# Own buffers for each pair's rows, norm and projections, and fewer VectorE steps for norm, rotary, softplus and factors, in a two-layer network of scan, experts and two attentions

## The chip, the cores and the metric

The kernel runs on one core of one Trainium2 chip. The time is the device time of one execution in microseconds (us), taken as the median of several runs. All arithmetic is float32, apart from a few masks and one-hot tables in bfloat16. The engines are named as in the profile: PE is TensorE (PEld its weight loads), DVE is VectorE, ACT is ScalarE, POOL is GpSimd, and SP is SyncE, which issues most DMAs.

## The reference

The input is 16 sequences of 256 rows with 128 features. Cut to what matters, this is computed:

```python
xn = layernorm(x)
x = x + mamba(xn) + experts(xn)          # block 0
xn = layernorm(x)
x = x + arccos_attention(xn) + window_layers(xn)   # block 1

mamba:   xt = silu(conv4(xn @ in_proj)); dt, B, C = split(xt @ x_proj)
         dt = softplus(dt @ dt_proj + dt_b)
         h[t] = exp(dt*A)*h[t-1] + dt*B*xt;  y = sum_n h*C + D*xt     # 256 channels x 16 states
         out = (y * silu(z)) @ out_proj
experts: top-1 of 8, relu(x @ w1 + b1) @ w2 + b2, times the gate's probability
arccos_attention, 16 heads of 8:  q, k = l2norm(q), l2norm(k)
         s = (1 + arccos(clip(q @ k.T))) ** -3.2;  n_r, n_c = row and column sums of s
         p = s / (n_r * n_c);  p = p / max(sum(p), 1e-12);  out = (p @ v) @ w_out
window_layers, 2 layers, 8 heads of 64:  h = shift(x)   # second 64 features one row later
         q, k, v = h @ wqkv;  q, k = rotary(l2norm(q)*qs), rotary(l2norm(k)*ks)
         x = x + softmax(window 64)(q, k) @ v @ wo
         h = layernorm(shift(x))*g + b;  a, g = h @ w1;  x = x + (a*gelu(g)) @ w2
```

## The kernel before

**Tiling.** The 16 sequences are taken as 8 pairs of 512 rows. A pair goes through block 0 (a scan over its 512 rows for 2 groups of 128 channels and 16 states, in 16 steps of 2 states each, and the experts, in 46 tiles of 128 routed rows of all pairs) and then through block 1: the arccos attention of the pair in 8 blocks of 4 heads, and two window layers for each of the two sequences, called b = 0 and b = 1.

**What sets the order.** The work is cut into units such as `("m_scan", pair, 0, step)` or `("ln", layer, b, 0)`. A unit is a chain of stages, each on one engine; `STAGES` gives the time that a planner assumes for each, `all_units` gives a wished time (`want`) and the units that must come first, and `schedule` plays all engines through once before the program is built: whenever an engine is free it takes the offered unit with the earliest wish. The result is one fixed order per engine, and a fixed PSUM bank per unit. On the chip each engine walks through its list in that order and waits at semaphores; nothing is reordered there. So the assumed times and the dependencies change the order, but a wait that comes late on the chip holds everything behind it on that engine.

**Streams.** Block 1 has three streams that run beside each other: the arccos attention (`g_...` units, ACT lines L1235 to L1255 for its logarithms, tangents and powers, POOL line L1721 for a subtraction of 2048 columns, called `g_sub`), and the window layers of b = 0 and of b = 1. Beside them runs the scan of a later pair (`m_...` units, DVE lines L1416, L1422, L1428). The experts (`e_...`) run in the first part only.

**Names on which the change acts.** For pair i:

- `f_yg` (POOL, L1717) gathers the expert rows into `yg`, which is the same memory as `sq`, the squares of the window layers' q and k. It therefore waits until all squares of pair i-1 are read (L1714). `f_ln` (DVE, L1442 to L1453) adds them to `x1` and takes the statistics, `f_xn` (L1463) writes the normalized rows `xn`, one buffer for all pairs, `f_tr` (L1469) copies their transpose to `xnT`, and `g_qkv` (L1473) adds the bias to q, k and v of the arccos attention in `gqkv`, one buffer as well. `g_sq` (L1211) squares q and k into `la[0]`, the tile in which the attention keeps its scores.
- `m_dt` is the softplus: DVE adds the bias (L1396) and forms -|x| (L1400), ACT takes Exp and Ln (L1182, L1184), and `m_du` on DVE (L1403, L1405) adds max(x, 0) and multiplies by xt.
- `qkv` of a window layer: DVE multiplies by the cosines (L1555), then the two swapped halves by the sines into `rb` (L1559, L1560), and sums the squares (L1562); POOL adds `rb` (L1725).
- `ln` and `ln2`: the second 64 features come shifted from PE into PSUM (L1093 to L1095), the first 64 stay in `xd`; DVE takes statistics of the four pieces (L1607, L1608), joins them (L1611), and normalizes the four pieces (L1619).
- `g_avT`: five DVE steps on 128x16 factors (L1520 to L1528) between the transposed product and its scaling (L1533).
- `shift` (ACT, L1272, L1273) writes the shifted transpose to `hT1`, which has memory of its own, with a column of zeros that is set once.

## Time and profile before

| what | value |
|---|---|
| median of 3 runs | 2691.4 us (2688.46 to 2696.2) |
| the profiled execution | 2701.68 us, its span 2700.4 us |
| busy PE / DVE / ACT / POOL | 2055.9 / 2026.8 / 1885.1 / 546.8 us |
| share of the span | 76% / 75% / 70% / 20% |
| mean granted TensorE clock | 0.806 of 2.4 GHz |

The profiled execution is 10 us above the median of the runs. Three engines are busy for about three quarters of the span each. The page's digits (busy tenths in 40 slices of 67.5 us) show where one of them is full: a 9 is 90% or more. The views used below are the page, windows of the span (busy time of each engine in a stretch), groups of instructions by line, one line's instructions, and the instructions in order of time.

### The profile page before, as it was taken

The numbers are of one execution on the slowest core, as the hardware profiler recorded it, in microseconds if no ns is written. First come the engines' busy times: TensorE is split into PE (matmuls) and PEld (weight loads), VectorE is DVE, ScalarE is ACT, GpSimd is POOL, SyncE is SP. The second block draws the span as 40 slices with busy tenths as digits, with TensorE's granted clock in tenths as the row PEclk, the third lists the DMA queues.
The fourth block names the chain that finished last, engine by engine and source line by source line (L and its number), as shares of the span: only waits on it lengthen the run. The fifth ranks groups of instructions, "written<-read, shape, count | busy, mean of one in ns | idle before, by whom it ended". The sixth has DMA issues, their size and how long they took to land.

```text
span 2700.4 us, 33039 instructions
## 1 busy us (share of the span) xinstructions
PE 2055.9 (76%) x10866; PEld 1355.6 (50%) x10866; DVE 2026.8 (75%) x3325; ACT 1885.1 (70%) x2742; POOL 546.8 (20%) x207
## 2 busy tenths in 40 slices
PE   4776788776877878878777868788777887777666
PEld 2533466642544555545444545455444555555445
DVE  4979963489789877888679876898589875564654
ACT  3435767655787678765877768875987667777775
POOL 2412121111221121221211112222221122212220
PEclk8886798887788878788868877889788877787878
DMA  7621124421101001110101001110101000000000
GB/s 251 226 83 47 47 86 123 129 73 63 40 32 53 19 5 52 32 47 13 37 24 55 24 4 37 39 52 16 37 32 48 24 4 1 1 5 5 1 1 5
DMA packets 67530, 126.32 MB, mean 47 GB/s; under 512 B 8836, under 2 KB 40132, under 8 KB 67236
## 3 DMA queue, kind: packets, MB, share of 16 engines
q1 hardware_dynamic: 61808, 113.19, 13.2%
q0 software_dynamic: 2816, 7.21, 0.8%
q10 hardware_dynamic: 2740, 3.80, 0.4%
q8 instruction: 92, 1.51, 0.2%
q14 instruction: 74, 0.61, 0.1%
HBM read 111.33 MB, written 12.85 MB: 46 GB/s over the span
## 4 chain that ended last, share of the span: by engine, by line
PE 32%; DVE 26%; ACT 21%; issue 16%; DMA 2%; SPq 1%; ACTq 1%; POOL 0%; DVEq 0%; POOLq 0%
PE ps L746 5%; PE ps L926 5%; DVE hB L1422 4%; ACT L741 4%; PE ps L968 3%; PE ps L1027 3%; PE ps L1052 3%; ACT arena L1243 3%; DVE hB L1428 3%; DVE hB L1416 2%; ACT arena L1253 2%; DVE n_c L1504 2%; PE ps L982 2%; ACT arena L1235 2%; ACT arena L1309 2%
## 5 line engine op out<-in xcount | busy, mean ns | idle before, releaser
L1721 POOL TENSOR_TENSOR arena<-arena 128x2048 f32<-128x2048 f32 x64 | 306.5, 4790 | 1272.0 <-ACT arena L1237 1272.0
L746 PE MATMUL ps<-w_ident,arena 128*128 128x128 f32 x1647 | 306.8, 323 | 147.4 <-DVE arena L1571 28.8
L926 PE MATMUL ps<-hB,w_ident 128*128 128x512 f32 x512 | 323.0, 765 | 99.3 <-DVE hB L1428 99.0
L746 PEld LDWEIGHTS ps<-w_ident,arena 128*128 128x128 f32 x1647 | 231.6, 169 | 255.1 <-issue 188.9
L1422 DVE TENSOR_TENSOR_SCAN hB<-dA,hB 128x1024 f32<-128x1024 f32 x128 | 322.0, 2518 | 1.9 <-ACT dA L1196 1.2
L1725 POOL TENSOR_TENSOR arena<-arena,rb 128x1024 f32<-128x1024 f32 x64 | 151.8, 2371 | 706.9 <-DVE rb L1560 706.9
L741 ACT ACT_TABLE_LOAD x189 | 242.5, 1283 | 19.7 <-issue 16.4
L1027 PE MATMUL ps<-w_l_wqkv,hT 128*128 128x512 f32 x384 | 223.6, 701 | 9.6 <-DVE lss L1562 5.8
L1196 ACT ACTIVATE dA<-dtv,w_A_log 128x510 f32<-128x510 f32 x256 | 168.8, 714 | 87.6 <-DVE hB L1422 85.1
L926 PEld LDWEIGHTS ps<-hB,w_ident 128*128 128x128 f32 x512 | 110.4, 237 | 217.0 <-issue 108.9
L1497 DVE TENSOR_SCALAR arena<-ps 128x512 f32<-128x512 f32 x256 | 163.9, 682 | 70.1 <-PE ps L968 70.0
L1309 ACT ACTIVATE arena<-ps,nmx 128x128 f32<-128x128 f32 (+1 forms) x512 | 159.0, 396 | 78.5 <-DVE nmx L1582 77.4
L1428 DVE TENSOR_TENSOR hB<-hB,BC 128x1024 f32<-128x1024 f32 x128 | 197.8, 1546 | 0.5
L1416 DVE TENSOR_TENSOR hB<-BC,du 128x1024 f32<-128x1024 f32 x128 | 180.3, 1413 | 22.4 <-PE ps L926 21.7
L1316 ACT ACTIVATE PT<-ps 128x384 f32<-128x384 f32 x256 | 124.6, 490 | 92.9 <-PE ps L746 92.1
L982 PE MATMUL ps<-arena,vt 128*32 128x256 f32 x1024 | 100.4, 527 | 116.3 <-DVE vt L1510 90.8
L1504 DVE TENSOR_REDUCE n_c<-arena 128x8 f32<-128x2048 f32 x64 | 146.0, 2281 | 55.5 <-ACT arena L1255 54.7
L968 PE MATMUL ps<-gqT,gkT 8*128 8x256 f32 x1024 | 174.6, 470 | 13.0 <-DVE arena L1497 5.3
L1052 PE MATMUL ps<-arena 64*128 64x128 f32 (+1 forms) x1024 | 163.3, 401 | 0.0
L1281 ACT ACTIVATE sq<-ps 128x512 f32<-128x512 f32 x128 | 76.3, 596 | 113.0 <-DVE lss L1562 77.5
L1555 DVE TENSOR_TENSOR arena<-ps,w_rot 128x512 f32<-128x512 f32 x128 | 87.5, 684 | 84.3 <-ACT sq L1281 84.2
L1235 ACT ACTIVATE arena<-arena,one_b 128x2048 f32<-128x2048 f32 x64 | 128.0, 2000 | 30.2 <-DVE arena L1497 26.6
(202 smaller groups left out, 4404.2 us busy)
## 6 DMA issues: line engine op xcount, KB each, us to landing
BC<-bc_d SPq DMA_DIRECT2D x128, 512.0 KB
BC<-in_experts SPq DMA_DIRECT2D x31, 514.0 KB
arena<-in_experts SPq DMA_DIRECT2D x15, 514.0 KB
arena<-in_x SPq DMA_DIRECT2D x8, 256.0 KB, 5.7
...
```

The source lines that it names most:

```text
L741: a.preload_act_table_set(names[0])
L746: return t.transpose(out_, in_, ident[0:k, 0:k])
L926: e = t.matmul(lb(), ident, hB[k % 2][:, j], start=q == 0 and j == 0, stop=q == NQ - 1 and j == NG - 1)
L968: e = t.matmul(lb(z)[:, kt * L:(kt + 1) * L], gkT[32 * hi:32 * hi + GD, hb, kt * P:(kt + 1) * P], gqT[32 * hi:32 * hi + GD, hb], start=Tru ...
L1027: t.matmul(lb(), hT1[:, b, tt * P:(tt + 1) * P], w_lqkv[:, l, w * INNER:(w + 1) * INNER], start=True, stop=True).then_inc(p_q[b], 1)
L1052: e = t.matmul(o_, q_, kT[head_rows(z), k, b * L + j0:b * L + (L if qt else P)], start=False, stop=True)
L1309: e = a.activation(sm[b][:, hh, at], lb(z)[:, cols], ACT.Exp, bias=nmx[b][:, qt, hh:hh + 1])
L1416: v.tensor_tensor(hB[k % 2], Bb[q % 2], bc(du[:, c:c + 1], [P, NG, T]), ALU.mult).then_inc(v_bx, 1)
L1422: v.tensor_tensor_scan(hf, flat2(dA[k % 2]), hf, 0.0, ALU.mult, ALU.add).then_inc(v_scan, 1)
L1428: v.tensor_tensor(hB[k % 2], hB[k % 2], Cb[q % 2], ALU.mult).then_inc(v_hc, 1)
L1504: v.tensor_reduce(n_c, la[m % 2].rearrange("p h (k s) -> p h k s", k=2), AX.X, ALU.add).then_inc(v_own, nv.up())
L1721: g.tensor_tensor(la[m % 2], la[m % 2], cl, ALU.subtract).then_inc(g_sub, 1)
```

## The change

It does six things.

1. `xn` gets two buffers, taken in turn by pairs. The expert rows of pair i are gathered straight into `xn[i % 2]`, and `f_yg` waits only for readers of pair i-2 (`wo`, `shift` and `f_tr` of i-2) instead of the last squares of pair i-1.
2. v of the arccos attention gets two buffers (`gv`), q and k one (`gqk`); `xnT` and the squares of q and k move into `cl`, the tile of cosines. So `g_qkv` of pair i no longer waits for the last `g_av` of pair i-1, while `f_tr` of pair i waits for the last `g_sub` of pair i-1, the last reader of `cl`.
3. `hT1` moves into `qT`. `shift` of a layer then waits for the scores of the layer before, and `heads`, which writes `qT`, for all six projections of its own layer; `shift` writes its column of zeros each time, one more small activation.
4. The softplus: max(x, 0) and |x| are two activations from PSUM (Relu and Abs with the bias) where DVE had two steps; Exp takes the sign.
5. The rotary swap is one DVE instruction over 512 columns with a reversed half index. `ln` brings the first 64 features into PSUM too (three matmuls of 64, 64 and 64 columns become 128, 128 and 64), so that statistics and normalization are two pieces of 128 columns instead of four of 64.
6. The factors of `g_avT` take three steps on 128x16 instead of five. The bias of `g_qkv` is added in two instructions where it was one, since q, k and v lie in two tiles.

The planner's table follows.

```diff
-    "m_dt": [("PE", 1.15), ("DVE", 1.5), ("ACT", 1.3)], "m_du": [("DVE", 1.6)],
+    "m_dt": [("PE", 1.15), ("ACT", 2.3)], "m_du": [("DVE", 1.3)],
...
-             *[("qkv", LAY * i - 1, b, k) for b in range(2) for k in (3, 4) if i])          # f_yg
+             *[(u, LAY * (i - 2), b) for b in range(2) for u in ("wo", "shift") if i >= 2],
+             *[("f_tr", i - 2) for z in range(1) if i >= 2])
...
-        unit(start - 20, ("f_tr", i), ("f_xn", i), *[("g_qkv", i - 1, 0, tt) for tt in range(TT) if i])
+        unit(start - 20, ("f_tr", i), ("f_xn", i), *[("g_sub", i - 1, 1, HB - 1) for z in range(1) if i])
...
-            unit(start, ("g_qkv", i, 0, tt), ("f_tr", i), *[("g_av", i - 1, 1, HB - 1) for z in range(1) if i])
+            unit(start, ("g_qkv", i, 0, tt), ("f_tr", i))
...
-                        x = [("down", n - 1, b)] if l else [("f_xn", i)] + [("qkv", n - 1, b, z) for z in range(6) if n]
+                        x = [("down", n - 1, b)] if l else [("f_xn", i)] + [("score", n - 1, b, 3) for z in range(1) if n]
...
-                        x = [("qn", n, b, k)]
+                        x = [("qn", n, b, k), ("qkv", n, b, 2), ("qkv", n, b, 5)]
...
+                    a.activation(dtv[:, k], lb(), ACT.Relu, bias=dt_b[:, k:k + 1])
...
+                    a.activation(tmp[:, k], lb(), ACT.Abs, bias=dt_b[:, k:k + 1]).then_inc(a_abs, 1)
...
+                    a.activation(hT1[b][64:128, 0:1], one_b[64:128, 0:1], ACT.Copy, scale=0.0)
...
-                    v.tensor_scalar(dtv[:, k], lb(), dt_b[:, k:k + 1], None, ALU.add).then_inc(v_own, nv.up())
...
-                    v.scalar_tensor_tensor(tmp[:, k], dtv[:, k], -1.0, dtv[:, k], ALU.mult, ALU.min).then_inc(v_spa, 1)
...
-                    v.tensor_tensor(gqkv[:, k], lb()[:, 0:3 * DM], b_gqkv[:], ALU.add).then_inc(v_gq, 1)
+                    v.tensor_tensor(gqk[:, k], lb()[:, 0:2 * DM], b_gqkv[:, 0:2 * DM], ALU.add)
+                    v.tensor_tensor(gv[i % 2][:, k], lb()[:, 2 * DM:3 * DM], b_gqkv[:, 2 * DM:], ALU.add).then_inc(v_gq, 1)
...
-                    v.tensor_tensor(rb[:, w, :, 0:H2], raw[:, :, H2:LD], bc(S[:, 0:H2].unsqueeze(1), [P, LH, H2]), ALU.mult)
-                    v.tensor_tensor(rb[:, w, :, H2:LD], raw[:, :, 0:H2], bc(S[:, H2:LD].unsqueeze(1), [P, LH, H2]),
-                                    ALU.mult).then_inc(v_rot[b], 1)
+                    v.tensor_tensor(rb[:, w].rearrange(halves, z=2), raw.rearrange(halves, z=2)[:, :, ::-1],
+                                    bc(S.rearrange("p (z e) -> p z e", z=2).unsqueeze(1), [P, LH, 2, H2]), ALU.mult).then_inc(v_rot[b], 1)
...
-                    v.reciprocal(rr, r[:, :, :, GD + 1]).then_inc(v_own, nv.up())
-                    v.tensor_tensor(dn, r[:, :, :, GD], rr, ALU.mult).then_inc(v_own, nv.up())
-                    v.tensor_scalar(dn, dn, 1e-12, None, ALU.max).then_inc(v_own, nv.up())
+                    v.tensor_scalar(rr, r[:, :, :, GD + 1], 1e-12, None, ALU.mult).then_inc(v_own, nv.up())
+                    v.tensor_tensor(dn, r[:, :, :, GD], rr, ALU.max).then_inc(v_own, nv.up())
                     v.reciprocal(dn, dn).then_inc(v_own, nv.up())
-                    v.tensor_tensor(dn, dn, rr, ALU.mult).then_inc(v_own, nv.up())
...
-                        v.bn_stats(lst6[:, 2 * b + h, 0], xd[:, 2 * b + h, 0:64]).then_inc(v_own, nv.up())
-                        v.bn_stats(lst6[:, 2 * b + h, 1], src[:, h]).then_inc(v_own, nv.up())
+                        v.bn_stats(lst6[:, 2 * b + h], half_of(lb())[:, h]).then_inc(v_own, nv.up())
...
-                        for x_, o_ in ((xd[:, z, 0:64], hn[b][:, h, 0:64]), (src[:, h], hn[b][:, h, 64:])):
-                            e = v.tensor_scalar(o_, x_, lst2[:, z, 0:1], lrstd[:, z:z + 1], ALU.subtract, ALU.mult)
+                        e = v.tensor_scalar(hn[b][:, h], half_of(bank(("ln", i, b, k)))[:, h], lst2[:, z, 0:1], lrstd[:, z:z + 1],
+                                            ALU.subtract, ALU.mult)
```

In all, DVE has 320 instructions fewer (3325 to 3005). ACT has 74 more: 32 of the softplus, 32 columns of zeros and 10 table loads (189 to 199), which the new order brings. POOL has one memset less, and PE's matmuls keep their number.

The new order moves the front of a pair. The first place is DVE around the rows of pair 4 (`x_0` is its `x1`), before: the sum and the statistics (L1445 to L1452) stand in the tail of pair 3, 245 rows behind the product that they wait for (L1439, row 1303).

```order
L1571 TENSOR_TENSOR arena<-arena,lss 128x1024 x2
L1601 TENSOR_TENSOR xd<-xd,ps 128x256
L1445 SCALAR_TENSOR_TENSOR x_0<-sq,prob,x_0 128x128 x4
L1449 BN_STATS st<-x_0 128x6 x4
L1452 BN_AGGR st<-st 128x2 x4
L1607 BN_STATS lst<-xd 128x6
```

After, on DVE, the same sum (now L1444, reading `xn`) comes 19 rows behind that product (now L1438, row 1152):

```order
L1613 TENSOR_SCALAR arena<-ps,w_l_ln_g,w_l_ln_b 128x256
L1444 SCALAR_TENSOR_TENSOR x_0<-xn,prob,x_0 128x128 x4
L1448 BN_STATS st<-x_0 128x6 x4
L1451 BN_AGGR st<-st 128x2 x4
L1493 TENSOR_SCALAR arena<-ps 128x512 x2
L1617 SCALAR_TENSOR_TENSOR arena<-ps,w_l_b,arena 128x256 x2
```

The copy of the transpose (L1469 before, L1463 after) then stands where `cl` is given back, ahead of the last column sums of pair 3's attention instead of behind them, and the projections follow at once:

```order
L1415 TENSOR_TENSOR hB<-BC,du 128x1024
L1463 COPY arena<-ps 128x512
L1421 SCALAR_TENSOR_TENSOR hB<-dA,hB 128x1024
L1467 TENSOR_TENSOR gqk<-ps,w_g_b_qkv 128x256
L1468 TENSOR_TENSOR gv<-ps,w_g_b_qkv 128x128
```

The second place is ACT at the softplus of pair 4, before: four activations (Exp and Ln for each channel group), with the bias and the sign done on DVE.

```order
L1225 ACTIVATE gqT<-ps 128x4x128
L1182 ACTIVATE hB<-hB 128x512
L1184 ACTIVATE hB<-hB,one_b 128x512
L1182 ACTIVATE hB<-hB 128x512
L1184 ACTIVATE hB<-hB,one_b 128x512
```

After, on ACT, each channel group takes four (Relu, Abs, Exp, Ln); the first group's stand here, ahead of a table load for the gelu:

```order
L1317 ACTIVATE arena<-ps,nmx 128x192
L1186 ACTIVATE dtv<-ps,w_dt_b 128x512
L1189 ACTIVATE hB<-ps,w_dt_b 128x512
L1191 ACTIVATE hB<-hB 128x512
L1193 ACTIVATE hB<-hB,one_b 128x512
L744 ACT_TABLE_LOAD
```

The window layers keep their place: between the last power of one pair's arccos attention and the first logarithm of the next stand 42 to 51 units of ACT's list before (pairs 2 to 7) and 26 to 39 after. The first unit of the last pair's window layers is number 1344 of ACT's 1511 units before and 1328 after.

## Rows read from the trace of the kernel before

**Rows 1.** The page: busy time of each engine; digits of DVE in 40 slices.
```profile
PE 2055.9 (76%) x10866; PEld 1355.6 (50%) x10866; DVE 2026.8 (75%) x3325; ACT 1885.1 (70%) x2742; POOL 546.8 (20%) x207
...
DVE  4979963489789877888679876898589875564654
```

**Rows 2.** Windows: us, then busy us (instructions) of PE, PEld, DVE, ACT, POOL, clock.
```profile
560.00:680.00 120.00, 81.50 (x290) 38.91 (x288) 115.58 (x110) 66.40 (x93) 16.73 (x4) 0.74 0.23 73
1204.00:1518.00 314.00, 242.36 (x1244) 152.43 (x1243) 259.25 (x397) 229.10 (x313) 62.13 (x20) 0.80 0.10 33
2199.00:2697.00 498.00, 357.30 (x2167) 253.08 (x2166) 276.08 (x585) 362.10 (x489) 99.99 (x32) 0.77 0.01 2
```

**Rows 3.** The page: the chain that ended last, by engine.
```profile
PE 32%; DVE 26%; ACT 21%; issue 16%; DMA 2%; SPq 1%; ACTq 1%; POOL 0%; DVEq 0%; POOLq 0%
```

**Rows 4.** In order of time, hand-over from pair 3 to 4: start, us, engine, line.
```profile
1278.38 0.69 DVE L1439 TENSOR_TENSOR x<-x,ps 128x512 f32<-128x512 f32 x1 [0.66 <-PE ps L934]
...
1503.85 1.91 ACT L1255 ACTIVATE arena<-arena 128x2048 f32<-128x2048 f32 x1
...
1507.32 0.96 POOL L1717 DMA_INDIRECT sq<-y_d,slot  x1 [0.16 <-issue]
...
1517.56 1.14 DVE L1445 SCALAR_TENSOR_TENSOR x<-sq,prob,x 128x128 f32<-128x128 f32 x4
...
1570.61 1.99 ACT L1235 ACTIVATE arena<-arena,one_b 128x2048 f32<-128x2048 f32 x1
```

**Rows 5.** Groups by line and form, DVE: busy us, mean ns, idle before and releaser.
```profile
L1555 DVE TENSOR_TENSOR arena<-ps,w_rot 128x512 f32<-128x512 f32 x128 | 87.5, 684 | 84.3 <-ACT sq L1281 84.2
L1559 DVE TENSOR_TENSOR rb<-ps,w_rot 128x256 f32<-128x256 f32 x128 | 52.9, 414 | 1.3 <-POOL arena L1725 1.3
L1619 DVE TENSOR_SCALAR arena<-xd,lst,lrstd 128x64 f32<-128x64 f32 x64 | 32.1, 501 | 4.2 <-ACT lrstd L1326 4.2
L1619 DVE TENSOR_SCALAR arena<-ps,lst,lrstd 128x64 f32<-128x64 f32 x64 | 21.6, 338 | 0.0
L1524 DVE TENSOR_SCALAR gfac<-gfac 128x16 f32<-128x16 f32 x32 | 20.3, 635 | 1.1
L1623 DVE TENSOR_SCALAR arena<-ps,w_l_ln_g,w_l_ln_b 128x256 f32<-128x256 f32 x32 | 17.3, 539 | 13.7 <-PE ps L746 13.6
L1473 DVE TENSOR_TENSOR gqkv<-ps,w_g_b_qkv 128x384 f32<-128x384 f32 x32 | 16.8, 549 | 8.6 <-PE ps L950 8.5
L1608 DVE BATCH_NORM_STATS2 lst<-ps 128x6 f32<-128x64 f32 x64 | 13.7, 214 | 0.0
L1631 DVE TENSOR_TENSOR xd<-xd,ps 128x256 f32<-128x256 f32 x32 | 13.3, 415 | 26.5 <-PE ps L1118 26.5
L1400 DVE SCALAR_TENSOR_TENSOR hB<-dtv 128x512 f32<-128x512 f32 x16 | 12.1, 755 | 0.5
L1396 DVE TENSOR_SCALAR dtv<-ps,w_dt_b 128x512 f32<-128x512 f32 x16 | 11.9, 745 | 21.0 <-PE ps L918 21.0
L1520 DVE RECIPROCAL gfac<-ps 128x16 f32<-128x16 f32 x32 | 8.0, 250 | 18.6 <-PE ps L746 18.5
L1449 DVE BATCH_NORM_STATS2 st<-x 128x6 f32<-128x128 f32 x32 | 7.0, 281 | 0.3
L1522 DVE TENSOR_TENSOR gfac<-ps,gfac 128x16 f32<-128x16 f32 x32 | 5.6, 174 | 1.1
```

**Rows 6.** The same view: ACT's groups, and PE's costliest.
```profile
L741 ACT ACT_TABLE_LOAD x189 | 242.5, 1283 | 19.7 <-issue 16.4
L1281 ACT ACTIVATE sq<-ps 128x512 f32<-128x512 f32 x128 | 76.3, 596 | 113.0 <-DVE lss L1562 77.5 <-PE ps L1027 34.2
L1326 ACT ACTIVATE lrstd<-lrstd 128x2 f32<-128x2 f32 x32 | 6.5, 203 | 1.0
...
L926 PE MATMUL ps<-hB,w_ident 128*128 128x512 f32 x512 | 323.0, 765 | 99.3 <-DVE hB L1428 99.0
```

**Rows 7.** One line's instructions, L1524: ns min/median/max.
```profile
L1524 DVE TENSOR_SCALAR gfac<-gfac x32: 174/175/3409, 283.6 to 2655.0; 128x16 f32<-128x16 f32 x32
```

121 lines of the change are left out of this document (55 added, 66 removed).

## The prediction

> **What bounds the kernel now.** I read the page's busy times first. PE, DVE and ACT are busy for 76%, 75% and 70% of the span, POOL for 20% [rows 1]: no single engine is full, and none is far from the others. The slices tell more. DVE's digit is 9 in eight of 40 slices [rows 1], 540 us in all, and those are stretches with the scan. From 560 to 680 us DVE is busy for 115.6 of 120 us while PE has 81.5 and ACT 66.4 [rows 2]: there DVE alone sets the pace. A whole middle pair, 1204 to 1518 us, has DVE at 259 of 314 us (83%), PE at 242 and ACT at 229 [rows 2]. Once the last scan is over, 2199 to 2697 us, the order turns round: DVE 276 of 498 us (55%), ACT 362 (73%), PE 357 (72%) [rows 2]. So DVE is the fullest engine in the middle and the emptiest of the three at the end.
>
> The chain that ended last goes through PE for 32% of the span, DVE for 26%, ACT for 21%, and 16% is issue [rows 3]. It changes engine all the time, which is what a fixed interleaving of several streams looks like. I use it as an exchange rate. DVE has 26% of 2700 = 702 us on the chain out of 2027 us busy, so a microsecond of DVE work taken away is worth 702/2027 = 0.35 us if it lies as DVE work lies on average. ACT's rate is 567/1885 = 0.30, PE's 864/2056 = 0.42.
>
> **What the change takes from DVE.** Durations are means of groups [rows 5].
>
> - Softplus: 16 times 745 + 755 ns (L1396, L1400), 24.0 us. The sum that is left in `m_du` (a tensor_tensor of 512 for a scalar_tensor_tensor) I take at the same price.
> - Rotary: 128 times, two of 414 ns (L1559, and L1560 like it) become one of 512 columns from PSUM. The nearest row has that very shape, L1555 with 684 ns: 128 x 0.144 = 18.4 us. That a reversed half costs nothing extra has no row; if it were read at half rate (684 ns more for one) the step would lose 128 x 0.54 = 69 us, which I think unlikely since the index only steps over blocks of 32 columns.
> - `ln`: four of 214 ns (L1608, and L1607 like it) become two of 281 ns (L1449): 0.294 us, 32 times, 9.4 us. The joins stay two, counted at nothing.
> - `ln2`: two of 501 and two of 338 ns (L1619) become two of 128 columns from PSUM. Between 64 columns (338) and 256 (L1623, 539) a column costs 1.05 ns, so 405 ns each: 1.678 - 0.810 = 0.868 us, 32 times, 27.8 us.
> - `g_avT`: 250 (L1520) + 174 (L1522) + 635 (L1524) + 250 + 174 = 1483 ns become 174 + 174 + 250 = 598 ns: 0.885 us, 32 times, 28.3 us.
> - Bias of `g_qkv`: 549 ns (L1473) become 415 (L1631, 256 columns) and, at 1.05 ns less a column, 281: 0.147 us more, 32 times, -4.7 us.
>
> Together 103.2 us, 5% of DVE's work.
>
> **What it adds.** ACT gets 32 activations of 512 columns from PSUM at 596 ns (L1281), 19.1 us, 32 columns of zeros at about 203 ns (L1326, two columns), 6.5 us, and 10 table loads at 1283 ns, 12.8 us [rows 6]: 38.4 us, 2% of its work. The softplus chain itself gets no longer: 1.50 us on DVE become 1.19 us on ACT. PE's three matmuls of `ln` move 128 columns more; at the 765 ns of a 512-column matmul (L926) [rows 6] these are 0.19 us at most, 32 times, 6 us, between 0 and 2.5 us on the chain, taken as 1.
>
> **What of it lies on the path.** By the exchange rate the gain is 103.2 x 0.35 = 35.7 us, the loss 38.4 x 0.30 = 11.6 us and 1: net -23 us. This is too low where DVE is full. The eight slices hold at least 0.9 x 540 = 486 us, 24% of DVE's work; if a quarter of the savings falls there at one for one and the rest at 0.35, the gain is 25.8 + 27.1 = 53 us, net -40 us. At the far ends, all of DVE's savings count and none of ACT's additions (-103 us), or the reverse (+38 us). I take the middle of the two central values, -31 us.
>
> One part of the 103 us is doubtful. L1524 has a mean of 635 ns, a median of 175 and a maximum of 3409 [rows 7], and L1619 on `xd` has 501 ns where the same shape from PSUM has 338 [rows 5]. So the two lose 32 x 0.46 = 14.7 us and 64 x 0.163 = 10.4 us in a few stretched executions, and not by their size. If the cause of the stretch meets the next instruction instead, 25 us of the 103 stay, 25 x 0.35 = 9 us of time. I keep that in the range. The Trainium skill names such a cause (page "SBUF — State Buffer", section "Who interferes with whom"): a VectorE copy or tensor_scalar within SBUF, or one with two SBUF inputs, shares a port pair with GpSimd, and the one that comes second waits until the other's whole instruction is over. The stretched forms here read SBUF alone, and their new forms read PSUM. By that rule the wait is only handed to the next such instruction, and the sum would be -22 us instead of -31 us. I can't tell from the trace of before how often the next one is of that kind.
>
> **The buffers.** Pair 4's rows are ready in `x1` at 1279 us (L1439), its experts' rows are gathered from 1507 us on, when the last squares of pair 3 are read (L1717), and only then does its sum run, at 1517.6 us (L1445) [rows 4]. That is 239 us of waiting for memory. It doesn't hold the window layers: their next layer needs the end of the layer before in any case, and in the new order they start where they did, 1328 instead of 1344 of 1511 units for the last pair. It does hold the arccos attention. Its last power of pair 3 ends at 1505.8 us and its first logarithm of pair 4 starts at 1570.6 us [rows 4], a hole of 65 us with 46 of ACT's units in it; 34 are left in the new order, so the hole should shrink to 65 x 34/46 = 48 us. That is 17 us for the attention at each of seven hand-overs. I count it at nothing in the time: in the middle the layers have no slack that it could give, and what follows it (`out`) waits for b = 1 as well. The new waits are `f_tr` for the last `g_sub`, `shift` for the scores before, and `heads` for the projections of v. The last two are met early in the order (the last projection of v stands 5 to 38 units ahead of `heads` on PE, the last scores at least 4 ahead of `shift` on ACT).
>
> **Rivals.**
>
> 1. *The attention paced the pairs.* If the hole is what the streams wait for, each of seven pairs gets 17 us shorter, 119 us, on top of part of the 31: about 2560 us. For it: DVE would then be busy for 259 - 13 of 297 us, 83% as today, so no engine forbids it. Against it: the window layers have hardly moved in the order, and they are the longer path through a pair.
> 2. *The relief is covered.* DVE gets emptier, but PE and ACT are as full as before and take its place as the one that comes last; or the in-order wait of `f_tr` on DVE for the last `g_sub` gives it back. Behind that wait scan steps are queued. To cancel the 31 us it would have to last 4.4 us at each of seven hand-overs; the longest stretch of L1524 is 3.4 us [rows 7], and POOL is idle for 80% of the time, so this is possible but not likely for all seven. Time: within 8 us of 2691.
> 3. *ACT becomes the bound, slower.* In the last 498 us ACT is the fullest engine already, and in the middle it stands at 73%. The softplus activations and table loads come where the exponentials of the scan are due; every microsecond that ACT is late there the scan on DVE waits. The price is up to 38.4 us in full while DVE's gain is worth only its rate less the handed-on stretches, 27 us: +11 us; with DVE's gain gone altogether, +38 us. I take 2712 us. It decides from the point where ACT's additions reach the chain at more than 0.95 (36 out of 38 us), three times today's rate. For it: the 10 table loads are added without any work done. Against it: the additions are 5 us a pair, of 314 us in which ACT is idle for 85 [rows 2].
> 4. *The reversed half is slow* (above): +69 us on DVE, at 0.35 some 24 us, so about 2685 us, or 2700 us with stretches handed on.
>
> **How the numbers follow.** The sum is against the profiled span of 2700.4 us; its execution is 10 us above the median, 0.4%, and the differences carry over: 2691.4 - 31 = 2660 us. Chances: the forecast (2635 to 2683 us) 0.53; the attention's gain, in full or in part, 2550 to 2635 us, 0.13; covered 0.13; slow reversed half 0.03; slower through ACT or a worse interleaving 0.18. Every edit of the table re-draws the order of 6800 steps, and a re-drawn order can be 20 us better or worse without a reason in the parts; that is in these bands too. The range of 8 in 10 reaches from 2610 us (part of the attention's gain) to 2712 us (ACT in the chain). Faster by over 0.3% (about what a measurement of this kernel can tell from no change) is below 2683 us: 0.68. Within 0.3%: 0.13. Slower by over 0.3%: 0.19.
>
> **What would show it.** DVE's busy time should fall by 78 to 104 us to about 1925 to 1950 us, ACT's rise to about 1923 us. No row for the two softplus steps, the one rotary row at 0.68 us, `ln2` near 0.41 us without stretched ones, and the factors at 0.17, 0.17 and 0.25 us. If the stretches are handed on, the scan's three DVE lines (L1416, L1422, L1428) get longer means. The sum of `x1` should stand within some us of its product, and the hole of the attention near 48 us. ACT's table loads count 199. The prediction is wrong if DVE's busy time falls as said and the middle pairs keep their 300 us, or if the hole closes and the pairs get shorter by it.

## The result, and the profile after

| what | before | after |
|---|---|---|
| median of 4 runs each | 2693.8 us (2688.46 to 2702.02) | 2599.25 us (2589.78 to 2608.75) |
| profiled execution, span | 2701.68 us, 2700.4 us | 2598.73 us, 2597.4 us |
| mean granted TensorE clock | 0.806 | 0.833 |

The ratio is 0.9646, with a 95% interval of 0.9603 to 0.969: 95 us faster, where 31 us were forecast, and below the range of 2610 to 2712 us. The direction was right, the size was not.

The page of after answers to [rows 1] and [rows 3]: busy times, the digits of DVE and ACT, and the chain.

```profile
PE 1987.9 (77%) x10866; PEld 1319.4 (51%) x10866; DVE 1942.8 (75%) x3005; ACT 1920.3 (74%) x2816; POOL 545.0 (21%) x206
...
DVE  4889973479879875998788866899799956555644
ACT  3537677766798698886877778786878777788785
...
PE 28%; DVE 28%; ACT 22%; issue 18%; DMA 2%; SPq 1%; DVEq 0%; ACTq 0%
```

DVE lost 84 us of busy time (78 to 104 forecast) and ACT gained 35 (38). PE lost 68 us, which the forecast didn't have. The span fell by more than DVE's busy time, so DVE stays at 75% of it, and ACT's share went from 70% to 74%. The streams are packed more densely, not only relieved of work.

The groups of DVE by line and form in after, which answer to [rows 5]; columns as there:

```profile
L1421 DVE TENSOR_TENSOR_SCAN hB<-dA,hB 128x1024 f32<-128x1024 f32 x128 | 337.1, 2635 | 6.0 <-ACT dA L1205 5.2
L1415 DVE TENSOR_TENSOR hB<-BC,du 128x1024 f32<-128x1024 f32 x128 | 196.1, 1537 | 18.2 <-PE ps L928 17.4
L1427 DVE TENSOR_TENSOR hB<-hB,BC 128x1024 f32<-128x1024 f32 x128 | 186.5, 1458 | 0.4
L1553 DVE TENSOR_TENSOR rb<-ps,w_rot 128x512 f32<-128x512 f32 x128 | 87.0, 679 | 0.1
L1564 DVE TENSOR_TENSOR arena<-arena,lss 128x1024 f32<-128x1024 f32 x64 | 85.5, 1368 | 6.5 <-ACT lss L1299 6.5
L1608 DVE TENSOR_SCALAR arena<-ps,lst,lrstd 128x128 f32<-128x128 f32 x64 | 23.1, 403 | 3.9 <-ACT lrstd L1334 3.8
L1599 DVE BATCH_NORM_STATS2 lst<-ps 128x6 f32<-128x128 f32 x64 | 15.7, 286 | 20.8 <-PE ps L1097 20.8
L1467 DVE TENSOR_TENSOR gqk<-ps,w_g_b_qkv 128x256 f32<-128x256 f32 x32 | 13.3, 417 | 2.1 <-PE ps L952 2.0
L1402 DVE TENSOR_TENSOR dtv<-dtv,hB 128x512 f32<-128x512 f32 x16 | 11.0, 688 | 17.6 <-ACT hB L1193 17.6
L1468 DVE TENSOR_TENSOR gv<-ps,w_g_b_qkv 128x128 f32<-128x128 f32 x32 | 9.0, 280 | 0.0
L1521 DVE RECIPROCAL gfac<-gfac 128x16 f32<-128x16 f32 x32 | 8.1, 253 | 1.1
L1519 DVE TENSOR_TENSOR gfac<-ps,gfac 128x16 f32<-128x16 f32 x32 | 5.6, 175 | 1.1
L1517 DVE TENSOR_SCALAR gfac<-ps 128x16 f32<-128x16 f32 x32 | 5.3, 165 | 15.6 <-PE ps L749 15.5
```

Every new form costs what the forecast gave it: rotary 679 ns (684), `ln2` 403 (405), statistics 286 (281), biases 417 and 280 (415 and 281), factors 165, 175 and 253 (174, 174 and 250).

The windows of after, from the last power of one pair's arccos attention to the first logarithm of the next and then the attention's blocks; the last but one is the hand-over of [rows 4]. Behind them, from before, the same hand-over and the blocks behind it. Columns as in [rows 2].

```profile
1131.00:1167.00 36.00, 32.66 (x241) 23.70 (x232) 31.49 (x57) 26.09 (x55) 0.00 (x0) 1.00 0.16 52
1167.00:1437.00 270.00, 209.55 (x1010) 133.59 (x1008) 226.73 (x297) 207.02 (x268) 60.61 (x19) 0.79 0.11 35
1437.00:1486.00 49.00, 43.08 (x254) 28.88 (x255) 43.45 (x69) 32.38 (x62) 2.37 (x1) 0.90 0.06 17
1486.00:1729.00 243.00, 192.33 (x1001) 124.97 (x1000) 177.97 (x278) 199.68 (x262) 60.50 (x20) 0.80 0.09 30
```

```profile
1506.00:1571.00 65.00, 53.46 (x316) 37.92 (x317) 56.80 (x109) 36.29 (x76) 11.12 (x7) 0.89 0.03 9
1571.00:1806.00 235.00, 184.39 (x912) 115.90 (x910) 181.20 (x280) 190.51 (x236) 55.72 (x18) 0.78 0.12 38
```

This hole went from 65 to 49 us (48 forecast); the seven together, measured the same way from the end of the last power to the start of the first logarithm, from 458 to 318 us. In this hole of before ACT is busy for 56% of the time (36.29 of 65 us), in the blocks behind it for 81% (190.51 of 235), while PE and DVE are above 80% in the hole: a hole is time in which ACT has too little to do and the other two are fuller. Over all seven holes of before and the blocks behind them ACT has 58% and 78%.

The instructions of after in order of time at the same hand-over answer to [rows 4]: the product, `x1`'s sum, the copy of the transpose, the bias, and the attention's last power and next first logarithm.

```profile
1226.52 0.69 DVE L1438 TENSOR_TENSOR x<-x,ps 128x512 f32<-128x512 f32 x1 [2.81 <-PE ps L936]
...
1244.98 1.13 DVE L1444 SCALAR_TENSOR_TENSOR x<-xn,prob,x 128x128 f32<-128x128 f32 x4
...
1418.98 0.68 DVE L1463 COPY arena<-ps 128x512 f32<-128x512 f32 x1
...
1422.26 0.42 DVE L1467 TENSOR_TENSOR gqk<-ps,w_g_b_qkv 128x256 f32<-128x256 f32 x1 [0.40 <-PE ps L952]
...
1435.12 1.91 ACT L1261 ACTIVATE arena<-arena 128x2048 f32<-128x2048 f32 x1
...
1485.78 2.00 ACT L1241 ACTIVATE arena<-arena,one_b 128x2048 f32<-128x2048 f32 x1
```

The sum comes 18 us behind its product where it was 239 us behind, and the projections' bias is added (from 1422 us on) before the last power (1435 us).

### The profile page after: what moved, and what is told of

The parts are those of the page before. It is cut to its first block, busy times and chain, and to the rows that moved or that the text cites. A ratio compares the mean times of both kernels' runs of the same rounds, so it can differ in the third digit from the quotient of the medians.

```text
span 2597.4 us, 32766 instructions
## 1 busy us (share of the span) xinstructions
PE 1987.9 (77%) x10866; PEld 1319.4 (51%) x10866; DVE 1942.8 (75%) x3005; ACT 1920.3 (74%) x2816; POOL 545.0 (21%) x206
## 4 chain that ended last, share of the span: by engine, by line
PE 28%; DVE 28%; ACT 22%; issue 18%; DMA 2%; SPq 1%; DVEq 0%; ACTq 0%
DVE hB L1421 5%; PE ps L749 5%; ACT L744 4%; PE ps L928 4%; DVE hB L1415 3%; PE ps L970 3%; DVE n_c L1500 3%; DVE hB L1427 3%; ACT arena L1241 3%; PE ps L984 2%; ACT arena L1249 2%; ACT arena L1317 2%; PE ps L1054 2%; PE ps L1089 2%; PE ps L1029 2%
## 5 line engine op out<-in xcount | busy, mean ns | idle before, releaser
L928 PE MATMUL ps<-hB,w_ident 128*128 128x512 f32 x512 | 316.3, 751 | 94.2 <-DVE hB L1427 93.2
L1421 DVE TENSOR_TENSOR_SCAN hB<-dA,hB 128x1024 f32<-128x1024 f32 x128 | 337.1, 2635 | 6.0 <-ACT dA L1205 5.2
L744 ACT ACT_TABLE_LOAD x199 | 255.3, 1283 | 15.7 <-issue 12.1
L1029 PE MATMUL ps<-w_l_wqkv,arena 128*128 128x512 f32 x384 | 214.4, 675 | 21.0 <-ACT arena L1280 8.2
L1493 DVE TENSOR_SCALAR arena<-ps 128x512 f32<-128x512 f32 x256 | 163.8, 682 | 75.4 <-PE ps L970 73.6
L1415 DVE TENSOR_TENSOR hB<-BC,du 128x1024 f32<-128x1024 f32 x128 | 196.1, 1537 | 18.2 <-PE ps L928 17.4
L1427 DVE TENSOR_TENSOR hB<-hB,BC 128x1024 f32<-128x1024 f32 x128 | 186.5, 1458 | 0.4
L970 PE MATMUL ps<-gqT,gkT 8*128 8x256 f32 x1024 | 163.4, 448 | 21.8 <-DVE lss L1555 9.2
L1073 PE MATMUL ps<-arena,PT 128*128 128x65 f32 x512 | 106.7, 295 | 90.3 <-ACT PT L1324 85.0
L984 PE MATMUL ps<-arena,vt 128*32 128x256 f32 x1024 | 91.3, 487 | 109.5 <-DVE vt L1506 88.5
L1073 PEld LDWEIGHTS ps<-arena,PT 128*128 128x128 f32 x512 | 93.9, 220 | 136.4 <-ACT PT L1324 103.2
```

The source lines that it names most:

```text
L744: a.preload_act_table_set(names[0])
L928: e = t.matmul(lb(), ident, hB[k % 2][:, j], start=q == 0 and j == 0, stop=q == NQ - 1 and j == NG - 1)
L970: e = t.matmul(lb(z)[:, kt * L:(kt + 1) * L], gkT[32 * hi:32 * hi + GD, hb, kt * P:(kt + 1) * P], gqT[32 * hi:32 * hi + GD, hb], start=Tru ...
L1029: t.matmul(lb(), hT1[b][:, tt * P:(tt + 1) * P], w_lqkv[:, l, w * INNER:(w + 1) * INNER], start=True, stop=True).then_inc(p_q[b], 1)
L1415: v.tensor_tensor(hB[k % 2], Bb[q % 2], bc(du[:, c:c + 1], [P, NG, T]), ALU.mult).then_inc(v_bx, 1)
L1421: v.tensor_tensor_scan(hf, flat2(dA[k % 2]), hf, 0.0, ALU.mult, ALU.add).then_inc(v_scan, 1)
```

## The experiments

Each group of kernels shares a chip, and the runs of the kernel before on it (its medians were 2697 to 2704 us). A change in us is the ratio less one, times 2697 us. The kernel after has an interval of 12 us either way, so a distance from it below that decides nothing; kernels on the same chip are compared directly. Busy times, holes and windows are those of one profiled execution of each kernel. All experiments compute the whole output.

### Which half brings it (four kernels, one chip)

**The steps alone.** Before, with parts 4 to 6 of the change (softplus, rotary and `ln`, factors) and their assumed times; all buffers and dependencies as before. The bias of `g_qkv` stays in one instruction here, since its split belongs to the two tiles.

```diff
-    "m_dt": [("PE", 1.15), ("DVE", 1.5), ("ACT", 1.3)], "m_du": [("DVE", 1.6)],
+    "m_dt": [("PE", 1.15), ("ACT", 2.3)], "m_du": [("DVE", 1.3)],
...
+                    a.activation(dtv[:, k], lb(), ACT.Relu, bias=dt_b[:, k:k + 1])
...
+                    v.tensor_tensor(rb[:, w].rearrange(halves, z=2), raw.rearrange(halves, z=2)[:, :, ::-1],
```

> The kernel before with the shorter softplus, rotary, norm and factor steps alone (parts 4 to 6 of the change, with their planner times), all buffers and dependencies as before. If the steps are worth their share of the chain (my prediction's rate), 20 to 40 us less than before, about 2660 us, and DVE busy 75 to 100 us less. If VectorE's work paced the pairs and the rate was too low, 60 us or more less. If the buffers bring all of the 95 us, within 15 us of before.

Measured: 2655.95 us, ratio 0.9843 [0.9816, 0.987], -42 us.

**The buffers alone.** After, with the old steps and their assumed times; parts 1 to 3 stay.

```diff
-                    t.matmul(half_of(lb())[:, :, 0:64], ident, xd[:, two, 0:64], start=True, stop=True)
+                    t.matmul(lb()[:, 0:64], w_next, xd[:, 2 * b, 64:], start=True, stop=True)
...
+                    v.tensor_scalar(dtv[:, k], lb(), dt_b[:, k:k + 1], None, ALU.add).then_inc(v_own, nv.up())
```

> The changed kernel with the old softplus, rotary, norm and factor steps: only the buffers, their dependencies and the column of zeros (parts 1 to 3). If the attention's hand-over paced the pairs (rival 1), 55 to 75 us less than before, and the hole between the last power of one pair and the first logarithm of the next is about 48 us as in the changed kernel. If the buffers are worth nothing by themselves, as the prediction counted, within 10 us of before although the hole shrinks.

Measured: 2636.66 us, ratio 0.9777 [0.9748, 0.9807], -60 us. The busy times on its page:

```profile
PE 1991.4 (76%) x10866; PEld 1318.4 (50%) x10866; DVE 2011.8 (77%) x3357; ACT 1883.6 (72%) x2768; POOL 546.1 (21%) x206
```

The two halves make -102 us, the whole change -95: they add up within the intervals. The steps brought some 10 us more than forecast, and the buffers, counted at nothing, brought 60. No large part of DVE's work is gone here (15 us of 2027), yet PE's busy time is 64 us lower. The seven holes sum to 341 us here and to 455 us with the steps alone.

**The planner's numbers.** Before with the assumed times of after, instructions unchanged; and after with those of before.

```diff
-    "g_ev": [("ACT", 0.5)], "g_avT": [("PE", 0.6), ("DVE", 1.5)], "g_oT": [("PE", 0.6), ("ACT", 0.5)],
+    "g_ev": [("ACT", 0.5)], "g_avT": [("PE", 0.6), ("DVE", 1.15)], "g_oT": [("PE", 0.6), ("ACT", 0.5)],
...
-    "ln2": [("DVE", 1.2)], "lnT": [("PE", 0.35), ("DVE", 0.45)], "up": [("PE", 1.25), ("ACT", 0.38), ("DVE", 0.42)], "down": [("PE", 1.8), ("DVE", 0.4)],
+    "ln2": [("DVE", 0.65)], "lnT": [("PE", 0.35), ("DVE", 0.45)], "up": [("PE", 1.25), ("ACT", 0.38), ("DVE", 0.42)], "down": [("PE", 1.8), ("DVE", 0.4)],
```

> The kernel before, every instruction the same, planned with the changed kernel's assumed times for shift, rotary, ln, ln2, factors and the sum of the softplus. It measures what a re-drawn order alone is worth. If the 95 us are no luck of the order, within 20 us of before (2675 to 2715 us). If the order's luck is a good part of them, 30 us or more off.

> The changed kernel, every instruction the same, planned with the old assumed times for shift, rotary, ln, ln2, factors and the sum of the softplus. If the gain is no luck of the order, 2585 to 2620 us. If the new table's order is a good part of it, 2630 us or more.

Measured: 2754.28 us, ratio 1.0211 [1.018, 1.0242], for before with the new numbers: 57 us slower with the same work. And 2630.22 us, ratio 0.9746 [0.9716, 0.9776], for after with the old ones: 27 us slower than after. Both lie outside what was expected if the order's luck is small. So the new numbers are no gain by themselves; of the two tables, each kernel is faster with the one that fits its own stages. That an edit of the table alone moves the time by 57 us also says how far a re-drawn order can go.

### Which dependency (four kernels, one chip)

**Late projections.** After, with buffers as they are, but the planner told to keep the old dependency of `g_qkv`.

```diff
-            unit(start, ("g_qkv", i, 0, tt), ("f_tr", i))
+            unit(start, ("g_qkv", i, 0, tt), ("f_tr", i), *[("g_av", i - 1, 1, HB - 1) for z in range(1) if i])
```

> The changed kernel with one more dependency in the planner: the arccos attention's projections of a pair come after the last g_av of the pair before, as in the kernel before. Buffers and instructions as changed; the rows' front stays early. If closing the attention's hole is what the buffers are worth, 2640 to 2665 us (40 to 60 us of the 61 us that the buffers alone gave are lost) and the hole back at 60 to 70 us. If the buffers help in another way (early rows, shift off the squares), 2585 to 2620 us though the hole is back.

**Late rows.** After, with the old dependency of `f_yg` on the last projections of pair i-1 added.

```diff
-             *[("f_tr", i - 2) for z in range(1) if i >= 2])
+             *[("f_tr", i - 2) for z in range(1) if i >= 2], *[("qkv", LAY * i - 1, b, k) for b in range(2) for k in (3, 4) if i])
```

> The changed kernel with one more dependency in the planner: the gather of a pair's expert rows comes after the last q and k projections of the pair before, as before. With it the sum, the norm, the transpose and with them the attention's projections are late. Both theories on the buffers expect a loss, about 2640 to 2665 us; if it is much worse than e5, the early rows have a worth beside the hole. If neither the hole nor the rows matter, 2585 to 2620 us.

Measured: 2670.09 us, ratio 0.989 [0.9874, 0.9907], and 2659.25 us, ratio 0.9855 [0.9839, 0.9872]. Either one alone takes back about all that the buffers brought: -30 and -39 us remain, about what the steps alone are worth (-42). Early rows without early projections bring nothing. The reverse can't be tried this way, since late rows hold back the projections too. The holes are back at 59 and 61 us on average (65 before, 45 after).

**DVE's steps in a fixed order.** To price DVE's time without a new order: before with the new rotary, `ln` and factors, but the old assumed times, so that every unit stands where it stood; and after with the same steps undone under its own times. (The softplus stays out, since it moves a unit between engines.)

```diff
-                    v.tensor_tensor(rb[:, w, :, 0:H2], raw[:, :, H2:LD], bc(S[:, 0:H2].unsqueeze(1), [P, LH, H2]), ALU.mult)
-                    v.tensor_tensor(rb[:, w, :, H2:LD], raw[:, :, 0:H2], bc(S[:, H2:LD].unsqueeze(1), [P, LH, H2]),
+                    v.tensor_tensor(rb[:, w].rearrange(halves, z=2), raw.rearrange(halves, z=2)[:, :, ::-1],
```

> The kernel before with the new rotary, norm and factor steps but the old planner times, so that every unit stands in the old order and only VectorE's steps get shorter (softplus as before). DVE loses about 79 us by the groups' means. At my rate of 0.35 that is 27 us, about 2667 us. If VectorE's time is dearer than the rate, 2655 us or less. If it is covered unless the order is drawn anew, 2685 us or more.

> The changed kernel with the old rotary, norm and factor steps executed in the new order (the planner still assumes the short ones). The same dose of VectorE work with the other sign. At the rate of 0.35, 27 us more than the changed kernel, about 2626 us. The buffers alone, planned with the true times of the old steps, took 2637 us: if 2650 us or more comes out, a plan that assumes too short times costs by itself, as e3 hints.

Measured: 2667.78 us, ratio 0.9891 [0.987, 0.9912], -29 us, as expected at the rate of 0.35; and 2646.41 us, ratio 0.9805 [0.9788, 0.9821], 43 us above after, where that rate gave 27. The second may hold some cost of a plan that assumes too short times, which no run separates. The busy times, in that order:

```profile
PE 2039.0 (77%) x10866; PEld 1348.0 (51%) x10866; DVE 1979.8 (74%) x3005; ACT 1883.6 (71%) x2742; POOL 548.8 (21%) x207
```

```profile
PE 2016.3 (76%) x10866; PEld 1339.0 (51%) x10866; DVE 1994.9 (75%) x3325; ACT 1920.8 (73%) x2816; POOL 543.9 (21%) x206
```

DVE's busy time moved by -47.0 and +52.1 us, so a microsecond of busy DVE is worth 29/47 = 0.6 and 43/52 = 0.8 us of time (32 and 47 us, or 0.7 and 0.9, by the medians themselves). Summed over the groups of the view by line (each group's busy time, close to the number times the mean by which the prediction counted), DVE's work moved by -75.4 and +78.4 us: 0.4 and 0.55 to 0.6. Below this is called summed durations. The two sums differ because neighbouring instructions of different groups overlap by some 0.09 us in the records (28 us over 320 instructions), and the engine's busy time counts an overlap once. Three rows in order of time, from after, show it: L1574 ends at 1146.54 us, and L1575 starts at 1146.46.

```profile
1146.12 0.42 DVE L1574 TENSOR_REDUCE nmx<-ps 128x2 f32<-128x256 f32 x1
1146.46 0.55 DVE L1575 TENSOR_REDUCE nmx<-ps 128x2 f32<-128x384 f32 x1
1146.92 0.48 DVE L1599 BATCH_NORM_STATS2 lst<-ps 128x6 f32<-128x128 f32 x2
```

### Which hand-over, and is it the hole (eight kernels, two chips)

The trace of the buffers alone had suggested that the first hand-over, from pair 0 to pair 1, carries much of the worth: its hole was 35 us shorter than before, more than any other.

**Early at the first hand-over only**, and **early at the later ones only**: both late dependencies put back for the other pairs.

```diff
-             *[("f_tr", i - 2) for z in range(1) if i >= 2])
+             *[("f_tr", i - 2) for z in range(1) if i >= 2], *[("qkv", LAY * i - 1, b, k) for b in range(2) for k in (3, 4) if i >= 2])
...
+            unit(start, ("g_qkv", i, 0, tt), ("f_tr", i), *[("g_av", i - 1, 1, HB - 1) for z in range(1) if i >= 2])
```

The second has `if i == 1` in both places.

> The changed kernel with the late rows and late projections of e5 and e6 as planner dependencies for pairs 2 to 7 only: the hand-over from pair 0 to 1 is as in the changed kernel, the six later ones as before. Theory A, from the traces: in e2 the attention of pair 1 starts 37 us earlier than in the kernel before and that shift lasts to the end, so the first hand-over, in a stretch where VectorE is half idle, makes most of the buffers' 61 us. Then about 2620 to 2630 us. Theory B, each hand-over is worth the same 9 us: about 2645 to 2655 us.

> The complement of e9: late rows and projections for pair 1 only, the six later hand-overs as in the changed kernel. Theory A: about 2630 to 2640 us (37 us lost). Theory B: about 2610 us (9 us lost).

Measured: 2671.82 us, ratio 0.9898 [0.9851, 0.9945], and 2600.78 us, ratio 0.9636 [0.959, 0.9683]. The two stand 71 us apart on one chip. The first hand-over is worth nothing that these runs can tell, the six later ones all: the theory from that trace falls. The other theory, 9 us for each hand-over, had the direction right and was too small as well: six times 9 us are 54, and giving up the six cost 68 us against after.

**All hand-overs earlier still.** After, with the front of the attention (projections, norm, heads and the first block of scores) wished for 60 us earlier, the transpose 40 us earlier.

```diff
-            unit(start, ("g_qkv", i, 0, tt), ("f_tr", i))
+            unit(start - 60, ("g_qkv", i, 0, tt), ("f_tr", i))
```

> The changed kernel with wished times 60 us earlier (transpose 40 us earlier) for the front of the attention: f_tr, g_qkv, g_sq, g_norm, the four g_hd of b = 0 and the first block's scores and logarithms. The planner then puts 13 to 20 of ACT's units in the hole where the changed kernel has 26 to 57. If the hole paces the pairs, it falls to about 25 us and the time to 2540 to 2575 us. If only what other work can't fill counts, 2585 to 2605 us: the layers are pushed back by what the attention gains.

Measured: 2650.98 us (2635.39 to 2670.88), ratio 0.9822 [0.9746, 0.9898], 50 us slower than the kernel with early later hand-overs on the same chip, though the seven holes now sum to 140 us. Both expected ranges were missed. The windows of pair 3 to 4, hole and blocks, in the kernel with the first hand-over only, with the later ones only, and with all earlier still. They are cut at the start of the last power's unit, 4 us ahead of its end, so the holes by the measure used above are 68, 49 and 22 us:

```profile
1445.00:1517.00 72.00, 59.37 (x312) 40.22 (x313) 63.36 (x110) 42.09 (x83) 13.69 (x7) 0.79 0.12 37
1517.00:1748.00 231.00, 173.48 (x941) 110.09 (x941) 192.77 (x257) 195.58 (x250) 54.91 (x16) 0.87 0.11 35
```

```profile
1439.00:1492.00 53.00, 44.83 (x265) 29.99 (x265) 47.50 (x74) 36.40 (x64) 2.37 (x1) 0.90 0.05 16
1492.00:1731.00 239.00, 187.34 (x971) 121.78 (x970) 173.46 (x272) 195.67 (x259) 61.34 (x20) 0.80 0.09 29
```

```profile
1457.00:1483.00 26.00, 21.20 (x141) 15.40 (x139) 23.69 (x34) 16.20 (x28) 2.35 (x1) 0.79 0.07 21
1483.00:1761.00 278.00, 217.03 (x1117) 138.93 (x1118) 225.29 (x323) 215.58 (x295) 59.05 (x19) 0.83 0.11 35
```

Hole and blocks together take 303, 292 and 304 us. In the first window of 72 us ACT is busy for 58%; with one of 26 us the time comes back in the blocks, where ACT falls from 82% (195.67 of 239) to 78% (215.58 of 278). That the blocks wait there for the work that the front was put ahead of is a guess. So the length of the hole is not itself what paces a pair.

**Another draw.** To see how much of all this is the luck of an order: after with `SWITCH`, what the planner adds to a unit's wish when the unit needs ACT to load another table, changed from 60 to 55 us.

```diff
-SWITCH = 60.0
+SWITCH = 55.0
```

> The changed kernel with nothing but the planner's penalty for a table switch changed from 60 to 55: another order, drawn with the same, true times. It measures the luck of an order. If the draws scatter little, 2590 to 2615 us; if e4's and e3's losses are only luck of that kind, 2620 us or more is as likely.

Measured: 2614.13 us, ratio 0.9691 [0.9644, 0.9739], 13 us above the kernel with the later hand-overs on the same chip.

**Where among the later ones.** The late dependencies for the last pair only (`if i == NPAIR - 1`), for pairs 2 to 6 only (`if 2 <= i < NPAIR - 1`), for pairs 2 to 7 with the switch at 55, and the front wished for 60 us earlier in the last pair only (each wish less `(60 if i == NPAIR - 1 else 0)`).

> The changed kernel with the late rows and late projections as planner dependencies for pair 7 alone; all pairs before keep the order of the changed kernel. If the last pair holds half of the buffers' worth, 2620 to 2645 us, all of the loss behind the end of pair 5. If the middle pairs hold it all, 2595 to 2610 us.

> The complement: late rows and projections for pairs 2 to 6, the last pair as in the changed kernel. If the worth is half in the middle, 2625 to 2645 us with pair 5 ending some 30 us later than in the changed kernel (2134 us); if it is all in the last pair, 2595 to 2610 us.

> e9 (late for pairs 2 to 7) planned with a penalty for a table switch of 55 instead of 60: another draw of the late order, as e12 is one of the early order. If the loss of e9 is its cause and not its draw, 2655 to 2685 us, as against 2599 to 2614 us for the early draws.

> The changed kernel with the attention's front wished 60 us earlier for pair 7 alone, where no scan runs that it could push back; the hole before it has 13 of ACT's units instead of 26. If the last pair is a chain that the attention's start sets, 2575 to 2590 us; e11 had 453 us from the end of pair 5 to the end, the changed kernel 460 us. If it isn't, 2595 to 2610 us.

| late where | median us | ratio | above after, us |
|---|---|---|---|
| last pair | 2617.0 | 0.9692 [0.9654, 0.9731] | 12 |
| pairs 2 to 6 | 2652.47 | 0.982 [0.9797, 0.9843] | 47 |
| pairs 2 to 7, switch 55 | 2651.92 | 0.982 [0.9797, 0.9843] | 47 |
| last pair 60 us earlier instead | 2611.87 | 0.9676 [0.9655, 0.9697] | 8 |

The middle pairs carry most of it, about 10 us each; the last pair's 12 us are at the edge of what can be told. With pairs 2 to 6 late, pair 5 ends at 2178 us where it ends at 2135 in after, 43 us later and not some 30. The sum, 59 us, is near the 68 us of all six together (the kernel with the first hand-over only, against after). The other draw with late dependencies is 35 us above the other draw without, but 21 us below the first draw with late ones and just under what was expected of it, so an order's luck is some 20 us and the split between the pairs is no finer than that. All kernels with the steps, the buffers and their own stages' times can be set side by side, leaving out the one with every front 60 us earlier and those with added work: the orders with an early front in the middle pairs took 2599 to 2617 us (five kernels), and those with a late one 2652 to 2672 us (five kernels). The effect is larger than what another draw cost or gave. Closing the last hole, to 16 us, didn't help either.

### What an engine's microsecond is worth (two kernels, one chip)

**ACT.** After with 128 more copies of 256 columns from PSUM to a spare tile, in the order of after.

```diff
+                        a.activation(spare, lb()[:, 0:L], ACT.Copy).then_inc(a_own, na.up())
```

> The changed kernel in its own order with 128 more ScalarE copies of 256 columns from PSUM into a spare tile (one ahead of every second PT copy), about 50 us of ScalarE work. If every engine's delay is passed on in a fixed interleaving, at a rate of 0.7 to 0.9 as VectorE's, 35 to 45 us more than the changed kernel, 2635 to 2645 us. At ScalarE's share of the chain (0.3), 15 us more. If VectorE alone paces the order, 5 us or less.

**PE.** After with two of the transposes of a stage made twice, 256 in all, in the order of after.

```diff
-                        for hp in range(LH // 2):
+                        for hp in [0, 1] + list(range(LH // 2)):
```

> The changed kernel in its own order with 256 more transposes of 128 columns on TensorE (two more in each half of the heads units, into the place that the next ones overwrite), 35 to 70 us of TensorE work. Passed on at 0.7 to 0.9: 25 to 60 us more than the changed kernel. At TensorE's share of the chain (0.37): 15 to 25 us more. If VectorE alone paces it, 5 us or less; less than nothing if the denser TensorE is granted more clock.

Measured: 2626.69 us, ratio 0.9726 [0.9705, 0.9747], and 2617.27 us, ratio 0.9692 [0.9675, 0.9709]. The group of the spare copies, in the view by line and form:

```profile
L1328 ACT ACTIVATE spare<-ps 128x256 f32<-128x256 f32 x128 | 48.9, 382 | 27.0 <-PE ps L750 26.6
```

and the two kernels' busy times:

```profile
PE 2008.4 (76%) x10866; PEld 1329.9 (51%) x10866; DVE 1941.0 (74%) x3005; ACT 1953.0 (74%) x2944; POOL 547.1 (21%) x206
```

```profile
PE 2017.0 (77%) x11122; PEld 1352.2 (52%) x11122; DVE 1943.0 (74%) x3005; ACT 1923.2 (74%) x2816; POOL 547.2 (21%) x206
```

The copies add 50 us of summed durations (33 us of busy time) on ACT and cost 22 to 27 us, by ratios or by medians: 0.45 to 0.55 of the summed durations. The transposes add 33 us to the groups' busy times on PE (29 us to PE's own) and cost 12 to 18 us: 0.4 to 0.55. With the interval of after counted in, ACT's price may be 0.2 to 0.7 and PE's anything up to 0.75. With DVE's 0.4 to 0.6, one price of about a half fits all three engines, but these runs don't show that the prices are equal. Neither 0.7 to 0.9 nor nothing fits ACT well; the transposes cost about what PE's share of the chain gave (15 to 25 us). The copies are spread differently from the softplus's activations, so this is a mean and not the price of that step.

## Why the prediction failed, and what of it held

**The step that failed.** "I count it at nothing in the time: in the middle the layers have no slack that it could give, and what follows it (`out`) waits for b = 1 as well." The sentence before it had the hole right: 17 us for each of seven hand-overs forecast, 65 to 48 us; measured 65 to 49, and 141 us in all. What was wrong was to see the window layers as one long path that only their own dependencies hold, with nothing to gain from an attention that starts earlier. The runs put -60 us on the buffers alone, 71 us between early and late hand-overs on one chip, and show the middle pairs as the main place. Why it is worth time is argued and not shown: the streams share engines that are each three quarters busy, and a longer stretch in which the attention feeds ACT may let the same work end sooner. Such an account could have been made from before's trace, by windows between the ends of a hole in [rows 4] and behind it: ACT does 0.56 us of work per microsecond in that hole and 0.81 in the blocks. The forecast's own 119 us less of hole are made up by 119 x 0.56/0.81 = 82 us more of blocks, net -37 us; by the 141 us measured it is -44. With the 58% and 78% of all seven holes and the blocks behind them it is -31 and -36. It falls short of the runs: with the buffers alone the holes shrank by 117 us, which gives -30 to -36 where -60 was measured. And with the holes down to 22 us it would promise more, and the run lost 50 us.

So the truth lies between the forecast and its first rival, whose full price, 2560 us, took all -119 us of the hole as time. The measured 2599 us lie in the band given to that rival in full or in part (2550 to 2635 us, 0.13). The rival holds by its direction and to half its size. The evidence set against it, that the window layers had hardly moved in the order (1344 to 1328 of 1511 units), said nothing on how fast the engines walk through that order.

**The steps.** Their net was -31 us; alone they brought -42 (interval about 7 us either way). Term by term, after against before: softplus 24.0 us (24.0 forecast), rotary 18.8 (18.4), `ln` with its joins 12.8 (9.4), `ln2` 30.6 (27.8), factors 28.5 (28.3), bias -5.5 (-4.7), 109 us for 103. All DVE groups together fell by 106.2 us, the busy time by 84.0, within the 78 to 104 forecast, but for another reason than the one given there: 22 us are overlaps of neighbours that went with the 320 instructions, and only 3 us net came back in forms that the change leaves alone.

**The exchange rates.** 0.35 for DVE and 0.30 for ACT came from each engine's share of the chain. Measured with the order kept: 0.4 to 0.6 and 0.45 to 0.55; PE's 0.42 lies within its 0.4 to 0.55. One of these four runs, the new steps in the old order, is no argument against 0.35: it took 2668 us for 2667 expected. With 0.5 for both, the steps make 112 us (DVE's summed durations in the kernel with the steps alone fell by that) less 28 us on ACT, times 0.5: -42 us, as measured; at 0.35 and 0.30 they make -31, outside the interval. Why the chain's share is too low no run shows; that it follows one path among many that are nearly as long is a guess. In the forecast itself the low rates nearly cancelled: 103 x 0.5 - 38 x 0.5 = -33 us. The higher central value, -40, came close by luck: it put a quarter of the savings at one for one, and no run shows that.

**Stretched instructions.** Two forms that read SBUF alone, L1524 and half of L1619, were stretched in before, and their new forms read PSUM: L1517 has a mean of 165 ns and L1608 one of 403, not stretched, though 11 of the 32 and 9 of the 64 ran while POOL was busy. All 10 stretched ones of L1524 in before did so too, and ended within 0.1 us of POOL's instruction. Whether the cause meets the next one instead can be read from lines that the change leaves alone. One line's instructions, min/median/max in ns, for the normalized rows before (L1463) and after (L1457), and for the last sum before (L1543) and after (L1536):

```profile
L1463 DVE TENSOR_SCALAR xn<-x,st,rstd x32: 336/342/349, 178.3 to 2394.1; 128x128 f32<-128x128 f32 x32
...
L1543 DVE TENSOR_TENSOR go<-go,xd x8: 691/692/693, 701.9 to 2697.4; 128x512 f32<-128x512 f32 x8
```

```profile
L1457 DVE TENSOR_SCALAR xn<-x,st,rstd x32: 315/338/3845, 175.4 to 2091.6; 128x128 f32<-128x128 f32 x32
...
L1536 DVE TENSOR_TENSOR go<-go,xd x8: 691/692/4028, 679.9 to 2594.4; 128x512 f32<-128x512 f32 x8
```

In order of time, after: the longest of them starts while POOL is in `g_sub` and ends with it, within 0.6 us.

```profile
1260.95 4.52 POOL L1713 TENSOR_TENSOR arena<-arena 128x2048 f32<-128x2048 f32 x1 [20.89 <-ACT arena L1243]
1261.99 4.03 DVE L1536 TENSOR_TENSOR go<-go,xd 128x512 f32<-128x512 f32 x1
```

With the order kept, forms that the change leaves alone got 15.7 us longer in before with the new steps (L1416 +10.0, L1422 +7.0), so about 16 of the 25 us in doubt were handed on; undoing the steps in after gave 10.7 us back. In the new order of after as a whole it was 3 us net: L1415 and L1421 31 us more, L1427, L1564 and L1433 32 us less. The forecast that all three scan lines get longer holds for two.

The Trainium skill states (page "SBUF — State Buffer", section "Who interferes with whom") that whoever issues first gets the shared port pair for its whole instruction and the other blocks. These rows agree: the sum that takes 0.69 us took 4.03 us behind a POOL instruction that had started first. That the wait then passes to the next instruction of its kind was the forecast's own step, and the 16 and 11 us bear it out in part. The sum of -22 us for the steps fails all the same: the handed-on part is at most 8 us of time by the price of a half, and other terms outweighed it.

**The rivals on the other side.** The waits of `f_tr` on DVE gave next to nothing back: L1463 of after sat idle for 2.1 us in all before its 8 copies. ACT did not become the bound: its busy time reached 1920.3 us (1923 forecast, 199 table loads as forecast), and added work on it cost about half of its durations. The one new wait that shows is L1402's 17.6 us for the softplus on ACT. The reversed half costs nothing extra, 679 ns for the 684 of the same shape unreversed.

**The test that the prediction set itself** reads "if the hole closes and the pairs get shorter by it", and that is what came in part: the holes shrank by 20 us each, and the pairs got shorter by half of that. Windows of pairs 2 to 5, from one pair's last sum to another's, before and then after:

```profile
1011.00:2222.00 1211.00, 959.04 (x4993) 615.56 (x4991) 988.58 (x1555) 906.65 (x1242) 250.47 (x80) 0.81 0.10 32
```

```profile
960.00:2134.00 1174.00, 928.88 (x4969) 606.71 (x4969) 956.28 (x1392) 922.12 (x1279) 249.91 (x80) 0.83 0.10 33
```

They take 37 us less, with ACT busy for 79% where it was 75%; 51 us are gained before them and 15 us behind. The first stretch of [rows 2], where DVE alone set the pace, is as full as it was: 118.67 of 120 us.

**The range.** It was stated that an order drawn anew can move the time by 20 us for no reason in the parts. The runs show 57 us for wrong assumed times, 27 for the reverse, and 13 and 21 us, one up and one down, for another draw with right ones. The range, down to 2610 us, counted the buffers' worth as a tail of 0.13, where two windows of the trace of before, hole and blocks, give it about half of the size it had.

**What stays open.** By what path an earlier attention shortens the middle pairs, since the account above covers about half of it; why closing the holes further lengthens the blocks; and whether PE's 68 us are in part a cause or only a consequence.
